# A decoder layer: cross-attention with projections in halves, and softmax sums inverted in a 64x64 tile

## The reference

```python
q = jnp.einsum('oc,bct->bot', Wq, target) + bq[None, :, None]
k = jnp.einsum('oc,bcs->bos', Wk, source) + bk[None, :, None]
v = jnp.einsum('oc,bcs->bos', Wv, source) + bv[None, :, None]
q = q.reshape(b, HEADS, HEAD_DIM, t)      # HEADS = 16, HEAD_DIM = 16; k and v too
dot = jnp.einsum('bhdt,bhds->bhts', q, k) / math.sqrt(HEAD_DIM)
mask = target_mask[:, :, :, None] * source_mask[:, :, None, :]
dot = mask * dot - (1.0 - mask) * NEG
amap = jax.nn.softmax(dot, axis=-1) * mask
out = jnp.einsum('bhts,bhds->bhdt', amap, v)
```

## Time and profile before

| | us |
|---|---|
| median of 3 runs | 2342.87 (2342.37 to 2356.09) |
| the profiled execution | 2321.17 |
| its span, first to last instruction | 2319.4 |
| cross-attention in it, first dot to last product | about 525 |
| mean granted clock of TensorE, share of full | 0.963 |

### The profile page before, as it was taken

How to read it: one execution, slowest core, us unless ns; L and a number is a source line. 1 busy time by engine, 2 the same in 40 slices (tenths; PEclk the granted TensorE clock), 3 DMA queues, 4 the chain that set the end, 5 groups by cost and what they waited for, 6 DMA issues and landing times. The chain is left out here.

```text
span 2319.4 us, 35373 instructions
## 1 busy us (share of the span) xinstructions
PE 2162.2 (93%) x11638; PEld 1521.2 (66%) x11638; DVE 1597.9 (69%) x2873; ACT 797.5 (34%) x1843; POOL 759.0 (33%) x531
## 2 busy tenths in 40 slices
PE   6899999999999999999999998879899989789998
PEld 4677777777777777777777876423333333267776
DVE  7658878878876558878888875657867878542221
ACT  1223323323323333223323322235555556652221
POOL 3234335335345234334335333212122221122211
PEclk9899999999999999999999999888978998999999
DMA  5211011011012111011011004745565444311100
GB/s 205 80 48 52 15 51 51 16 49 51 16 49 100 56 47 53 7 58 51 9 56 51 26 10 72 121 79 98 103 104 97 68 91 80 101 59 55 55 36 19
DMA packets 58564, 141.87 MB, mean 61 GB/s; under 512 B 9022, under 2 KB 23558, under 8 KB 53478
## 3 DMA queue, kind: packets, MB, share of 16 engines
q1 hardware_dynamic: 56726, 138.42, 23.7%
q10 hardware_dynamic: 1744, 2.25, 0.3%
HBM read 89.53 MB, written 17.29 MB: 46 GB/s over the span
## 5 line engine op out<-in xcount | busy, mean ns | idle before, releaser
L1638 DVE TENSOR_REDUCE x_mx<-x_pm 128x1 f32<-128x512 f32 x512 | 317.6, 682 | 77.3 <-PE x_pm L1731 74.4
L1493 ACT ACTIVATE x_E<-x_pd 128x512 f32<-128x512 f32 x512 | 265.0, 603 | 178.4 <-PE x_pd L1745 177.3
L1091 PE MATMUL a_pj<-q_big,a_wqk_h 128*128 128x512 f32 x1024 | 290.0, 405 | 0.5 <-POOL a_wqk_l L631 0.5
L1107 PE MATMUL a_pj<-a_wvg_h,q_big 128*128 128x512 f32 x1024 | 285.6, 406 | 1.1 <-DVE a_rm L789 1.0
L1107 PEld LDWEIGHTS a_pj<-a_wvg_h,q_big 128*128 128x128 f32 x1024 | 185.2, 188 | 51.8 <-DVE a_rm L789 2.4
L789 DVE TENSOR_TENSOR a_rm<-a_pj,a_rope 128x1024 f32<-128x1024 f32 x128 | 155.7, 1218 | 78.8 <-PE a_pj L1091 77.5
L1091 PEld LDWEIGHTS a_pj<-q_big,a_wqk_h 128*128 128x128 f32 x1024 | 183.0, 188 | 40.3 <-POOL a_wqk_l L631 1.3
L520 ACT ACTIVATE a_v<-a_pj 128x256 f32<-128x256 f32 x128 | 49.2, 384 | 414.8 <-PE a_pj L1107 414.8
L663 POOL TENSOR_TENSOR a_ogl<-a_ogf,a_ogh 128x512 fp32r<-128x512 f32 x62 | 79.3, 1302 | 281.8 <-ACT a_ogf L557 281.8
L1759 PE MATMUL x_pa<-x_E,x_vx 128*32 128x512 f32 x1024 | 154.3, 678 | 0.0
L866 DVE TENSOR_TENSOR a_acc<-a_po,a_acc 128x512 f32<-128x512 f32 x128 | 86.0, 687 | 88.6 <-PE a_po L1220 88.6
(11 more groups left out here) (220 smaller groups left out, 4618.4 us busy)
## 6 DMA issues: line engine op xcount, KB each, us to landing
a_qk_raw<-in_wqk SPq DMA_DIRECT2D x16, 1024.0 KB, 5.3
...
```

Source lines behind the costliest of these rows:

```text
L1091: last = mm(pj[:, j % 2, :], wa[:, c, j * P:(j + 1) * P], xa[:, c, p * UT:(p + 1) * UT], start=k == 0, stop=k == 11)
L1107: last = mm(pj[:, tt % 2, :], xa[:, c, t0:t0 + P], wa[:, c, :], start=k == 0, stop=k == 11)
L1493: nc.scalar.activation(E[:, n % ESLOTS, :], pd[:, n % 3, :], ACT.Exp, scale=XD ** -0.5).then_inc(exp_done, 1)
L1638: nc.vector.reduce_max(mx[:, u % 2, at:at + 1], pm[:, k % 3, :], AX_X).then_inc(pm_done, 1)
```

## The change

It does five things, all in the cross-attention.

- Each projection is cut in two (`project_part`): for q and k the two halves of the contraction, for v the two halves of the bank. The twelve halves stand in G4 to G15, between the first and the second pair of dots; VectorE's take-over stands in the odd steps, between its first and second pair of maxima, and ScalarE's `high` in G6, G8, G10 and G12.
- The sums go back once for each head and query, as 64 partitions of 64 columns (`compact`), into a tile that shares its allocation with `mT`. VectorE inverts that 64x64 tile in one instruction (G3, G12), SyncE writes it to DRAM (`publish`, G5, G14) and reads it into `sums` with each row repeated 16 times (`bring_back`, G7 and the next G0). The last half of the last batch keeps the old way.
- The twelve stack DMAs of a batch stand in other steps, G9 to G15 and G0, G1 of the next batch. For batch 1 only the six of Q are issued ahead of the loop, those of K in G1 to G3.
- x and mask are loaded one batch earlier: three loads ahead of the stage, then batch b + 3 in G15. The context load goes from G3 to G1, the stores to G5 and G13, the statistics to G1, the normalisation to G6.
- GpSimd takes three low parts, not two, ahead of the second division.

```diff

         def maxima_slot(u, q, i):

-            return 17 * u + 4 * q + i
+            k = 4 * q + i
+            return 17 * u + k - (u > 1 and k < 2)

         def turned_slot(u):

-            return 17 * u + 16
+            if u == 0:
+                return 16
+            return 17 * u + 18 - 2 * (u == QUADS - 1)

...
+        def compact(n):
+
+            return mT_cs[64:128, 64 * (n % 2):64 * (n % 2) + 64].bitcast(F32)
+
         def halved(b, w):
...
         def inverses(b, G):

-            if b + 2 < B:
-                due = {7: (-1, (0, 1)), 8: (-1, (2,)), 9: (-1, (3,)), 10: (0, (0,)), 11: (0, (1, 2)), 12: (0, (3,))}
-            else:
-                due = {**{2 + i: (-1, (i,)) for i in range(4)}, **{10 + i: (0, (i,)) for i in range(4)}}
-            n, parts = due.get(G, (0, ()))
-            return 2 * b + n, (parts if 2 * b + n >= 0 else ())
+            due = {3: -1, 12: 0} if b + 1 < B else {3: -1, 11: 0}
+            return (2 * b + due[G],) if G in due and 2 * b + due[G] >= 0 else ()
+
+        def published(b, G):
+
+            due = {5: -1, 14: 0} if b + 1 < B else {5: -1, 12: 0}
+            return (2 * b + due[G],) if G in due and 2 * b + due[G] >= 0 else ()
+
+        def returned(b, G):
+
+            due = {0: -2, 7: -1} if b + 1 < B else {0: -2, 7: -1, 13: 0}
+            return (2 * b + due[G],) if G in due and 2 * b + due[G] >= 0 else ()
...
-        FILLS = {10: ((1, 0), (1, 1)), 11: ((1, 4), (1, 5)), 12: ((0, 0), (0, 1)), 13: ((0, 2),), 14: ((0, 3), (1, 2)), 15: ((1, 3), (0, 4))}
-        LATE = {0: ((0, 5),)}
-        WHOLE = tuple((w, k) for w in range(2) for k in range(6))
+        FILLS = {9: ((1, 0),), 10: ((1, 1), (1, 4)), 11: ((1, 5),), 12: ((1, 2), (1, 3)),
+                 13: ((0, 0),), 14: ((0, 1), (0, 2)), 15: ((0, 3),)}
+        LATE = {0: ((0, 4),), 1: ((0, 5),)}
+        FIRST = tuple((0, k) for k in range(6))
+        SECOND = {1: ((1, 0), (1, 1)), 2: ((1, 4), (1, 5)), 3: ((1, 2), (1, 3))}
...
+                if n < 2 * B - 1:
+                    sp.dma_start(compact(n)[32 * k:32 * k + 32], raw[1:P:32, u % 2]).then_inc(sums_out[k], 16)
+                else:
+                    sp.dma_start(sums[64 * k:64 * k + 64, n % 2], raw[1:P:2, u % 2]).then_inc(sums_out[k], 16)
+
+            def publish(n):
+                sp.wait_ge(inv_done, n + 1)
+                sp.dma_start(inv_dram[n].rearrange("h (c t) -> (h c) t", c=8), compact(n)).then_inc(inv_out, 16)
+
+            def bring_back(n):
+                sp.wait_ge(inv_out, 16 * n + 16)
+                after(sp, x2_done, n - 1)
+                sp.dma_start(sums[:, n % 2], inv_dram[n].rearrange("h (o t) -> h o t", o=1).to_broadcast([8, XD, 512])).then_inc(inv_in, 16)
...
+                    if b and G in (5, 13):
+                        store(2 * b - 2 + (G == 13))
+                    for n in published(b, G):
+                        publish(n)
+                    for n in returned(b, G):
+                        bring_back(n)
+                    if b + 1 < B:
+                        stack(b + 1, (LATE if b else SECOND).get(G, ()))
                     if b + 2 < B:
-                        if G == 2 and b:
-                            load_x(b + 2)
-                        if G == 3:
+                        if G == 1:
                             load_c(b + 2)
                         if G in (6, 7):
                             mask_rows(b + 2, G - 6)
                         stack(b + 2, FILLS.get(G, ()))
+                    if G == 15 and b + 3 < B:
+                        load_x(b + 3)
...
-                    for i in range(4):
-                        exponent(16 * t + 4 * q + i)
+                    G = 4 * (t % 4) + q
+                    exponent(16 * t + 4 * q)
+                    exponent(16 * t + 4 * q + 1)
+                    if G in (6, 8, 10, 12) and t // 4 + 2 < B:
+                        high(t // 4 + 2, order(2)[G // 2 - 3])
+                    exponent(16 * t + 4 * q + 2)
+                    exponent(16 * t + 4 * q + 3)
                     if q == 0 and t:
                         take_weighted(t - 1)
-                    G = 4 * (t % 4) + q
-                    if 8 <= G < 12 and t // 4 + 2 < B:
-                        high(t // 4 + 2, order(2)[G - 8])
...
-            def invert(n, i):
+            def invert(n):
                 for k in range(2):
                     dve.wait_ge(sums_out[k], 16 * n + 16)
-                part = sums[:, n % 2, i * P:(i + 1) * P]
-                nc.vector.reciprocal(part, part).then_inc(inv_done, 1)
+                nc.vector.reciprocal(compact(n), compact(n)).then_inc(inv_done, 1)
...
+                    G = 4 * (t % 4) + q
+                    if u < QUADS:
+                        row_max(u, q, (0, 1))
                     if q == 0 and u <= QUADS:
                         max_rows(u - 1)
+                    if G in range(5, 16, 2) and b + 2 < B:
+                        take_projection(b + 2, order(2)[G // 2 - 2])
                     if u < QUADS:
-                        row_max(u, q)
-                    G = 4 * (t % 4) + q
-                    n, parts = inverses(b, G)
-                    for i in parts:
-                        invert(n, i)
+                        row_max(u, q, (2, 3))
+                    for n in inverses(b, G):
...
+            def project_part(b, j, k):
+                if k == 0:
+                    if j == 0:
+                        after(pe, xn_done, 2 * b - 2)
+                    if j == 2:
+                        pe.wait_ge(c_in, 16 * b)
+                    after(pe, pp_done, projected(b, j) - (b < 2))
...
+                    last = mm(dst[:, 0, :], w[:, k, (j % 2) * P:(j % 2 + 1) * P], src[:, k, :], start=k == 0, stop=k == 1)
...
+                        last = mm(dst[:, 0, k * 256:(k + 1) * 256], cx[:, c, q * P:(q + 1) * P], wv_t[:, c, :],
+                                  start=c == 0, stop=c == 1)
+                if k:
+                    last.then_inc(pp_ready, 1)
...
                 for q in range(4):
-                    for i in (0, 2):
-                        dot(t, q, i)
-                        dot(t, q, i + 1)
-                        if i + q == 0 and u <= QUADS:
-                            turn_max(u - 1)
-                        if u < QUADS:
...
                     G = 4 * (t % 4) + q
-                    if 7 <= G < 13 and b + 2 < B:
-                        project(b + 2, order(2)[G - 7])
+                    dot(t, q, 0)
+                    dot(t, q, 1)
+                    if u < QUADS:
+                        row_scores(u, q, 0)
+                        row_scores(u, q, 1)
+                    if G >= 4 and b + 2 < B:
+                        project_part(b + 2, order(2)[G // 2 - 2], G % 2)
+                    if q == 0 and u <= QUADS:
+                        turn_max(u - 1)
+                    dot(t, q, 2)
+                    dot(t, q, 3)
+                    if u < QUADS:
+                        row_scores(u, q, 2)
+                        row_scores(u, q, 3)
```

88 lines of the change are left out of this document (38 added, 50 removed).

## The result

The changed kernel takes **2269.3 us** (median of 4 runs, 2264.1 to 2279.55) against 2349.15 for the kernel before (median of 4, 2342.37 to 2356.09): a ratio of 0.9665, 95% interval 0.9614 to 0.9716. Forecast were 2287 and a range from 2243 to 2326. The profiled execution took 2264.1 us, with a span of 2262.3; before, it was 2321.2.

What follows compares the result with a forecast made beforehand. TensorE is busy 93% of the span; a batch is steps, waits and clock. The cross-attention stage falls from 525.2 to 477 us, 48 less, plus 7 for clock: 2342.9 - 48 - 7, say 2287 us, range 2243 to 2326.

Steps and rivals of the forecast that it cites:

- The step with a half: Steps G4 to G15 of a projecting batch: 2.94 - 0.21 + 0.96 = 3.69 us, or 4.07 at G4, G8, G12.
- The wait behind the backlog: At G4 of batches 1 to 5, row and context late behind stack pieces: 0.3 + 2.4 = 2.7 us a batch.
- at no cost: Statistics to G1, normalisation to G6, ScalarE's copies to even steps: no time added, since ScalarE and GpSimd have room.
- My own queue sum: Pieces at 2.2 us, store 0.7, x and mask load 1.9, last part 2.5: G1's row lands at G13 + 23.6.
- Batch 0: First batch: the 14.13 us row wait goes, a new 3.5 at G5 comes; 60.5 us, 63.5 with 3 for the clock.
- Batch 6: First batch without projections: 4 x 3.39 + 12 x 2.94 + 1.2 = 50 us.
- Inverses: On VectorE, eight reciprocals a batch become two of 64 columns at 0.5 us each; VectorE loses 6.4 us a batch.
- Clock: Half-clock spells after most waits cost 3 us a batch; fewer waits give back a third of 21.7 us, 7.
- The queue keeps up: Rival, chance 0.25: no wait at G4 or in batch 0, no slow-clock spells; stage 85 us less, 2258 or 2243.
- The halves hide nothing: Rival, chance 0.12: the half projections in the steps hide nothing, 16 us less gain; 2303 us.
- The backlog's 11 us bound: Rival, chance 0.12: waits at G4 of 11 in place of 2.7 us a batch cost 41 us; 2328 us.
- Long spells: Rival, chance 0.05: each large G4 wait is followed by the longest half-clock spell, 13 in place of 3; 2378 us.

Runs made afterwards that it cites:

- experiment 6: The changed kernel with each of the twelve half projections behind both pairs of dots, and VectorE's take-over behind the maxima: 2326.19 us, ratio 0.9931 to the kernel before.
- experiment 7: The changed kernel with six whole projections between the pairs of dots in the odd steps G5 to G15: 2301.21 us, ratio 0.9793 to the kernel before.
- experiment 1: The changed kernel with the statistics in G4 instead of G1 and GpSimd's first division ahead of the inverse root: 2287.75 us, ratio 0.9772.
- experiment 2: The changed kernel with the rows of maxima issued from ScalarE's DMA queue in place of SyncE's: 2270.86 us, ratio 0.972.
- experiment 5: The changed kernel with four reciprocals of 128 columns again and no way through DRAM: 2287.05 us, ratio 0.9755.
- experiment 3: The changed kernel with the edits of experiment 1 and experiment 2 together: 2274.12 us, ratio 0.9734.
- experiment 4: As experiment 3, with the x, mask and context loads also issued by ScalarE, in G1: 2266.88 us, ratio 0.9691.
- experiment 10: The changed kernel with five Q pieces moved to the next batch's G2 to G4, rows on ScalarE's queue, GpSimd reordered, statistics in G3: 2235.59 us, ratio 0.9532.
- experiment 11: As experiment 10, with the context load at G0 and, in batch 0, K pieces ahead and Q pieces in G2 to G4: 2234.01 us, ratio 0.9601.
- experiment 12: As experiment 11, with the statistics split, first half in G3 and the rest in G4: 2219.17 us, ratio 0.951.
- experiment 8: The kernel before with only the changed start, three early x loads and batch 1's K pieces in G1 to G3: 2323.28 us, ratio 0.9991.

## Why the prediction was right, and where it wasn't

- **Direction, size and range: right**, 18 us above the measured time. That the stage fits to 2.4 us (474.6 against 477) is luck: batch 0 came out 5.5 us shorter, batches 1 to 5 5.9 shorter, batches 6 and 7 9.0 longer, and within batches 1 to 5 steps 20 us too long hide waits and clock 14 us too short.
- **The step with a half was mis-sized: 3.39, not 3.69** (G8 3.68, not 4.07). I took from a plain step only the 0.21 us that it shows as idle. Its true slack stood in the earlier trace rows: at half clock TensorE is busy for 100% of a 4.6 us step, so it needs 2.3 us at full clock, and 0.64 of the 2.94 are hold-up, most of it inside matmuls that are shown as busy. 2.3 + 0.96 = 3.26, near the 3.39. A batch without waits is 53.8 us, not 57.8; over six batches 24 us too much. Experiments 6 and 7 show the mechanism itself to be as described: the place between the pairs hides the half, and halving lets it be hidden in every step.
- **The wait behind the backlog: right in kind, wrong in place and size.** I moved the statistics "at no cost", from G5 and G6 to G1, and named ScalarE and GpSimd as the work that has room, but did not ask what the statistics read. My own queue sum answers most of it. Six pieces stand ahead of the load: 1604.5 + 13.2, a store 0.7, the load 1.9, its last part 2.5, together 1622.8. VectorE needed it at 1619.8 and began at 1624.72, when the mask had landed; x had landed at 1622.4. So 3 of the 5 us followed from the numbers in hand. The wait then hid the one that I had put at G4, which experiment 1 brings back at 7.4 us. In all, batches 1 to 5 lost 311.6 - 5 x 53.8 = 42.6 us to waits and clock, 8.5 each, where I had 5.7. (Of my 2.7 us at G4 the 0.3 was a slip: the same lines give 23.6 - 23.5 = 0.1, and the wait for the context overlaps it.)
- **Batch 0: 58.0, not 63.5.** The 14.13 us went as said. The context and K pieces cost nothing at G4 that can be seen, and of the 3.5 us at G5 for VectorE's overwriting of K's source nothing came. But VectorE's statistics in G1 held TensorE for a moment, and the clock was at 0.50 from 1501.8 to 1512.0.
- **Batch 6: 58.6, not 50.** The late row of G1 was foreseen for batches 1 to 5 and not for batch 6, whose queue has the same pieces ahead. Experiment 2 takes it away and gives 49.6.
- **Inverses: right.** 550 ns against the 500 taken, and experiment 5 puts their part at some 3.2 us a batch. The reason given was weaker than the result: maxima of one shape, 512 columns, can't show a fixed part. GpSimd waits for the returned inverses (100 us in 10 waits), and TensorE, VectorE and SyncE do not wait for it.
- **Clock: too little, both ways.** The 3 us a batch were low where a wait struck. "The rows here agree", that each wait throws the clock back, was read too strongly: the 1.28 us at 1852.09 cost nothing. And the runs of the kernel before lie 28 us (median) above its profiled one, those after 5: 23 us went there, not 7. How much of the 23 is the draw of one profiled run stays open. The mean granted clock of a whole run was 0.963 to 0.971 after the change, and 0.934 to 0.968 in the runs of the kernel before beside the experiments.
- **Rivals.** "The queue keeps up" is refuted by experiments 1, 3 and 4; experiments 10 to 12 are what a queue that keeps up looks like, 2219 to 2236. "The halves hide nothing" is refuted by 6, where they do hide nothing and a step takes 3.99 us. The backlog's 11 us bound came true only in part (a G2 of 10.4 costs 7.4, slow clock included). Long spells were seen in experiments 1, 7 and 8 (30.7, 34.1 and 44.4 us at most); after this change the longest was 17.1.
- **The rule of the Trainium skill** (DMA: Bandwidth & Descriptors, Anatomy of one DMA) would have had the load of x and mask, 768 KB together, land in some 4 us, an estimate from its fixed 2.0 us and 436 GB/s. The page gives it for DMAs that GpSimd issues; here SyncE issues them, which neither the prediction nor this estimate allows for. In experiment 12, with no backlog ahead, the load nearly did: 3.7 us for x, 4.6 for the mask. Behind the stack pieces of the changed kernel it took 9.1 and 11.1.
- **Not run alone:** the other order of the stack pieces. It ended the waits of 1.26 to 1.31 us at each G0 and moved others; what it gives without the halves isn't known.
